# A graph network on one core: rows for the aggregations fetched per block in edge order, or not at all

## The reference

```
h   = relu(layernorm(x))
agg = segment_sum(h[src], dst)            # 1st aggregation
h2  = relu(agg / max(cnt, 1) @ W1l.T + b1 + h @ W1r.T)
agg = segment_sum(h2[src], dst)           # 2nd aggregation
x   = x + agg / max(cnt, 1) @ W2l.T + b2 + h2 @ W2r.T
h   = relu(layernorm(x))
x   = x + segment_mean(relu([h[src], h[dst], e] @ W1 + b1) @ W2 + b2, src)   # edge layer
```

## Time and profile before

| | us |
|---|---|
| three runs | 4372.95, 4394.75, 4398.56 |
| median | 4394.75 |
| span of the profiled execution | 4375.3 |

### The profile page before, as it was taken

How to read it: one execution, slowest core, us unless ns; L and a number is a source line. 1 busy time by engine, 2 the same in 40 slices (tenths; PEclk the granted TensorE clock), 3 DMA queues, 4 the chain that set the end, 5 groups by cost and what they waited for, 6 DMA issues and landing times. The chain is left out here.

```text
span 4375.3 us, 174335 instructions
## 1 busy us (share of the span) xinstructions
PE 3697.5 (85%) x64703; PEld 3536.1 (81%) x64703; DVE 3679.1 (84%) x6413; ACT 2589.0 (59%) x5168; POOL 3032.7 (69%) x2760
## 2 busy tenths in 40 slices
PE   3699999999977999999758888888888888888876
PEld 3688888888877999999747887877788887788876
DVE  7799999999988888888758888887878878888876
ACT  3455555555545666666537666666666666666664
POOL 1688888888854666666517777777777777777771
PEclk9899999999999999999868999999999999999998
DMA  5233333333326545555335555555555555555552
GB/s 104 68 84 83 83 82 83 83 83 85 82 64 170 118 118 118 118 118 119 68 110 162 163 169 175 174 159 159 164 166 174 174 162 161 160 165 174 174 153 65
DMA packets 481209, 557.42 MB, mean 127 GB/s; under 512 B 180610, under 2 KB 437873, under 8 KB 480870
## 3 DMA queue, kind: packets, MB, share of 16 engines
q1 hardware_dynamic: 395782, 451.91, 36.7%
q0 software_dynamic: 84032, 103.47, 10.2%
q10 hardware_dynamic: 1266, 0.31, 0.0%
HBM read 478.48 MB, written 76.90 MB: 127 GB/s over the span
## 5 line engine op out<-in xcount | busy, mean ns | idle before, releaser
L1388 POOL DMA_INDIRECT sorted_edges<-edge_rows,edge_index x1566 | 1535.3, 980 | 568.0 <-issue 559.1
L969 POOL DMA_INDIRECT conv_got<-parts_table,conv_index x1060 | 1324.5, 1250 | 467.2 <-issue 235.7
L1079 ACT CAST conv_rows<-conv_rows_ps 128x384 bf16<-128x384 f32 x2226 | 1020.3, 458 | 671.4 <-PE conv_rows_ps L993 654.8
L993 PE MATMUL conv_rows_ps<-parts,conv_hot_t 128*128 128x192 bf16 x8268 | 1049.8, 246 | 72.4 <-DVE conv_hot_t L1145 72.4
L1010 PE MATMUL conv_sums<-conv_rows,conv_hot_d 128*128 128x193 bf16 (+1 forms) x8268 | 1052.6, 247 | 3.0 <-DMA conv_got<-parts_table,conv_index 3.0
L993 PEld LDWEIGHTS conv_rows_ps<-parts,conv_hot_t 128*128 128x128 bf16 x8268 | 696.4, 97 | 94.7 <-issue 55.4
L1450 PE MATMUL edge_sums<-edge_parts,edge_hot 128*128 128x64 bf16 (+1 forms) x15582 | 597.2, 200 | 201.0 <-DVE acc L1640 196.7
L1450 PEld LDWEIGHTS edge_sums<-edge_parts,edge_hot 128*128 128x128 bf16 x15582 | 556.8, 102 | 220.9 <-DVE acc L1640 165.0
L1010 PEld LDWEIGHTS conv_sums<-conv_rows,conv_hot_d 128*128 128x128 bf16 x8268 | 720.4, 98 | 4.2 <-DMA conv_got<-parts_table,conv_index 3.7
L1435 PE MATMUL edge_a_ps<-parts,edge_hot_t 128*128 128x64 bf16 x15582 | 548.7, 197 | 36.4 <-issue 25.3
L1145 DVE TENSOR_SCALAR conv_hot_t<-conv_slot_row,node_of 128x768 bf16<-128x768 bf16 (+1 forms) x1484 | 542.1, 407 | 22.0 <-PE conv_rows_ps L993 14.6
(11 more groups left out here) (193 smaller groups left out, 4717.5 us busy)
## 6 DMA issues: line engine op xcount, KB each, us to landing
edge_slot_row<-slot_rows SPq DMA_DIRECT2D x371, 224.0 KB
edge_edges<-sorted_edges SPq DMA_DIRECT2D x371, 224.0 KB
conv_slot_row<-slot_rows SPq DMA_DIRECT2D x424, 192.0 KB
conv_slot_row<-slot_rows SPq DMA_DIRECT2D x318, 160.0 KB
edge_dst_row<-dst_rows SPq DMA_DIRECT2D x261, 192.0 KB
edge_attr<-in_edge_attr SPq DMA_DIRECT2D x260, 192.0 KB
sorted_edges<-edge_rows,edge_index POOLq DMA_INDIRECT x1566
conv_got<-parts_table,conv_index POOLq DMA_INDIRECT x1060
```

The costliest lines, as they stand in the source:

```text
L969: pool.indirect_dma_start(got[g][:, f, 0:PARTS * D], None, k.parts_table, bass.IndirectOffsetOnAxis(ap=index[h][:, g, at:at + 1], axis=0)) ...
L993: mm = pe.matmul(rows_ps[(bs * h + i) % banks][:, at:at + PARTS * D], hot_t[home[g]][:, v, u * P:(u + 1) * P], k.parts[:, 2 * (GU * g + u) ...
L1079: act.copy(rows[i % bufs][:, 0:n, 0:PARTS * D], rows_ps[(bs * h + i) % banks][:, 0:n * PARTS * D].rearrange("p (u d) -> p u d", u=n)).then ...
L1388: pool.indirect_dma_start(k.sorted, bass.IndirectOffsetOnAxis(ap=index[h][0:used, at:at + 1], axis=0), rows[j][0:used, t, :], None).then_i ...
```

## The change

Blocks are of two kinds. In a block of kind P no rows are fetched: all 49 units are expanded by PE. In a block of kind F nothing is expanded: GpSimd fetches all 3,840 rows by 30 indirect DMAs, one for each tile of 128 edges in their original order, and PE only reduces, 60 matmuls. `WHOLE` gives the pattern: conv1 alternates P, F (27 and 26 blocks), conv2 goes P, P, F (36 and 17 blocks). For an F block `hot_d` is made from `picked`, the destination numbers in edge order with those of unslotted edges set to zero. `index` holds all row numbers of the F blocks, made by two DVE instructions at the start; the fetches have five `got` tiles of seven, seven, seven, seven and two rows of tiles, each in one buffer that comes free when its group of the F block before has been reduced. In conv1 those tiles, `index` and `picked` lie in the room of `k.x`, and SP loads that part of x anew (72 of 98 windows) at the end. Sorting goes on for every block. The loops run over six blocks; POOL's stream is written out without a loop.

The diff, cut to its core:

```diff
-FETCHED = 2
+WHOLE = {"conv1": "PF", "conv2": "PPF"}
+ROUND = 6
@@ Sorting
+    def choose_dst(self, dve, c, f, picked):
+        k = self.k
+        link(dve, dve.scalar_tensor_tensor(self.at[:], self.rank[:], float(SRC_WINDOWS), k.src_window[:, bass.ds(c, 1), :].rearrange("p c t -> p (c t)"), ALU.mult, ALU.add), self.at_made, f + 1)
+        dve.scalar_tensor_tensor(picked[:, bass.ds(f, 1), :].rearrange("p f t -> p (f t)"), self.at[:], float(SLOTS),
+                                 k.dst_no[:, bass.ds(c, 1), :].rearrange("p c t -> p (c t)"), ALU.is_lt, ALU.mult).then_inc(self.dst_chosen, 1)
@@ conv
-        fetched = [1 + g % 2 for g in range(NG)]
-        steps = [[(u, min(u + 2, GU - n)) for u in range(0, GU - n, 2)] for n in fetched]
-        bs, cut, banks, bufs, most = NG * ns, 8, 2 if sorting else 3, 3, (GU - min(fetched)) * P
+        steps = [(u, min(u + 2, GU)) for u in range(0, GU, 2)]
+        bs, cut, banks, bufs = NG * ns, 10, 2 if sorting else 4, 4
...
+        room = k.x[:].rearrange("p w d -> p (w d)").bitcast(BF16)[:, 0:of_x] if sorting else o.tmp("room", [P, of_x], BF16)[:]
+        got = [room[:, g * a_got:(g + 1) * a_got].rearrange("p (u d) -> p u d", u=GU) for g in range(WG)]
@@ sync
+                if sorting:
+                    s.store_row(sp, t.b)
+                if t.kind == "F":
+                    return
...
+            if sorting:
+                sp.wait_ge(s.row_stored, 16 * NB)
+                sp.wait_ge(reduced, Turn(kinds, whole[-1]).made + WG)
+                sp.dma_start(k.x[:, 0:x_taken, :], k.x_rows[:, 0:x_taken, :]).then_inc(x_back, 16)
+                sp.wait_ge(x_back, 16)
@@ gpsimd
-            def number_rows(b, h, n):
...
+            pool.wait_ge(begun, 2)
+            pool.wait_ge(index_made, 1)
+            for f, b in enumerate(whole):
+                for g in range(WG):
+                    if f >= 1:
+                        pool.wait_ge(reduced, Turn(kinds, whole[f - 1]).made + g + 1)
+                    for t in tiles_of(g):
+                        pool.indirect_dma_start(got[g][:, t - GU * g, 0:PARTS * D], None, k.parts_table, bass.IndirectOffsetOnAxis(ap=index[:, f, t:t + 1], axis=0)).then_inc(got_landed[g], 16)
@@ tensor
+            def reduce_whole(t, g):
+                pe.wait_ge(hot_d_made, t.made + g + 1)
+                pe.wait_ge(got_landed[g], 16 * len(tiles_of(g)) * (t.f + 1))
+                if g == 0:
+                    sums_free(t)
+                for x in tiles_of(g):
+                    mm = add_up(t, g, x - GU * g, got[g][:, x - GU * g, 0:wide_cols])
+                mm.then_inc(reduced, 1)
...
+                for i in range(cut):
+                    if t.kind == "P":
+                        expand(t, i)
+                    if i < 2 and t.n >= 1 and last.kind == "P":
+                        rest_of(last, bs - 2 + i)
+                    if i >= 2 and t.kind == "P":
+                        reduce(t, i - 2)
+                    if i in (3, 8) and t.kind == "F":
+                        reduce_whole(t, i // 5)
+                    hooks(i, last, t, t1, t2)
+            def second(last, t, t1, t2, t3):
+                for j in range(3):
+                    if t.n >= 0 and t.kind == "F":
+                        reduce_whole(t, 2 + j)
+                    if j < 2 and sorts(t2) and (t.n < 0 or t.kind == "F"):
+                        s.prefix(pe, t2.b, t2.n, 1 + j)
@@ vector
+            at = slice(whole[0], NB, len(kinds))
+            link(dve, dve.scalar_tensor_tensor(node, k.src_window[:, at, :], float(SW), k.src_no[:, at, :], ALU.mult, ALU.add), node_made, 1)
+            dve.tensor_scalar(index, node, 1.0, float(ROWS - 1), ALU.subtract, ALU.min).then_inc(index_made, 1)
             if not sorting:
-                units = k.slot_src[:].rearrange("p b (g u) -> p b g u", u=GU)[:, :, :, GU - FETCHED:GU]
-                dve.tensor_tensor(row_of[:], units, wide(k.first_row[:], 1, [P, NB, NG, FETCHED]), ALU.add).then_inc(rows_numbered, 1)
+                dve.scalar_tensor_tensor(picked, k.place[:, at, :], float(SLOTS), k.dst_no[:, at, :], ALU.is_lt, ALU.mult).then_inc(all_picked, 1)
```

More of the change, by code:

```diff
@@ L906, in in_turn, with at @@
-            for b in range(2 * pairs, NB):
-                second(b, b % 2, MANY)
-                if b + 1 < NB:
-                    first(b + 1, (b + 1) % 2, MANY)
-        def sorts(b, lag):
-            return sorting and (not isinstance(b, int) or 0 <= b + lag < NB)
+            def at(c, i=None):
+                return [Turn(kinds, c + d, i) for d in (-1, 0, 1, 2, 3)]
+            for c in range(-ahead, 1):
+                first(*at(c))
+                if c < 0:
+                    second(*at(c))
@@ new lines, in in_turn, with here @@
+            second(*at(0))
+            first(*at(1))
+            second(*at(1))
+            first(*at(2))
+            with eng.Fori(0, rounds) as i:
+                for r in range(ROUND):
+                    second(*at(2 + r, i))
+                    first(*at(3 + r, i))
+            for c in range(2 + ROUND * rounds, NB):
+                second(*at(c))
+                if c + 1 < NB:
+                    first(*at(c + 1))
+        def here(t):
+            return not t.known or 0 <= t.b < NB
@@ new lines, in sums_free, with add_up @@
+            def sums_free(t):
+                if t.n >= 2:
+                    pe.wait_ge(summed, t.b - 1)
+            def add_up(t, g, u, row):
+                for v in range(2):
+                    mm = pe.matmul(sums[t.h][:, v * wide_cols:(v + 1) * wide_cols], hot_d[home_d[starts[t.c % len(kinds)] + g]][:, u, v * P:(v + 1) * P], row,
+                                   start=(g == 0 and u == 0 and v == 0), stop=(GU * g + u == t.units - 1), skip_group_check=True)
+                return mm
@@ L1069, in _ @@
+            in_turn(pe, first, second)
+            last = Turn(kinds, NB - 1)
+            if last.kind == "P":
+                for i in (bs - 2, bs - 1):
+                    rest_of(last, i)
+            move(last)
             if sorting:
@@ L1154, in take, with make_hot @@
-            def take(b, h, n):
-                dve.wait_ge(reduced, NG * b + NG)
-                dve.tensor_scalar(moved_to[:], k.iota[:], k.shift_to[:, bass.ds(b, 1)], None, ALU.is_equal)
-                both = sums[h][:, 0:2 * wide_cols].rearrange("p (v d) -> p v d", v=2)
+            def make_hot(t, g):
+                if t.kind == "P":
+                    dve.wait_ge(landed[g], 16 * (t.p + 1))
+                    if not t.known or t.p >= 1 or g >= since[g]:
+                        dve.wait_ge(expanded, ns * (NG * t.p + g + 1 - since[g]))
+                    for v in range(2):
+                        last = dve.tensor_scalar(hot_t[home[g]][:, v, :], slot_row[lane[g]][:], k.node_of[:, v:v + 1], None, ALU.is_equal)
+                    last.then_inc(hot_t_made, 1)
+                if g == 0:
+                    dve.wait_ge(dst_ready, t.b + 1)
+                x = starts[t.c % len(kinds)] + g
+                if not t.known or t.made + g >= since_d[x]:
+                    dve.wait_ge(reduced, t.made + g + 1 - since_d[x])
+                same_number(dve, hot_d[home_d[x]], k.nodes_b[:] if sorting else nodes_ps[:, 0:SW // 2].bitcast(BF16), dst_of[t.h], g, t.units).then_inc(hot_d_made, 1)
@@ L1159, in take @@
+            def take(t):
+                dve.wait_ge(reduced, t.made + t.groups)
+                dve.tensor_scalar(moved_to[:], k.iota[:], k.shift_to[:, bass.ds(t.b, 1)], None, ALU.is_equal)
+                both = sums[t.h][:, 0:2 * wide_cols].rearrange("p (v d) -> p v d", v=2)
                 if sorting:
@@ new lines, in second @@
+            def second(last, t, t1, t2, t3):
+                for g in range(3, NG):
+                    if t.n >= 0 and g < t.groups:
+                        make_hot(t, g)
+                    if g - 3 in range(t2.sums) and sorts(t2):
+                        s.plane(dve, t2.b, t2.h, t2.n, g - 3, t2.sums)
+                    if g == 4 and t.n >= 1:
+                        add(last)
+                    if g == 4 and not sorting:
+                        add_bias(t)
+                    if g == 5 and sorts(t2):
+                        s.choose(dve, t2.b, t2.n)
+                    if g == 6 and sorts(t2):
+                        s.sum_chosen(dve, t2.b, t2.n)
+                    if g == 5 and sorting and t.known and t.b == NB - 2:
+                        s.put_places(dve)
+                if here(t1):
+                    make_hot(t1, 0)
+                if sorts(t2):
+                    s.spread_rank(dve, t2.b)
+                    if t2.kind == "F":
+                        s.choose_dst(dve, t2.b, t2.f, picked)
```

430 lines of the change are left out of this document (192 added, 238 removed).

## The result

The kernel after took 4418.36 us (median of 19 runs), the kernel before 4372.95 us (19 runs on the same chip). The ratio, formed over the runs and not from the two medians, is 1.0081 (95% interval 1.0063 to 1.0100): slower by 35 us, against the forecast of 83.

A forecast was written before the change was run, and what follows sets the result against it. PE and DVE together bound conv1 and PE alone conv2; POOL was to become conv1's chain. conv1 +173 and conv2 -90 sum to +83 us, added to the median 4394.75: 4478 us, range 4350 to 4600.

The forecast's parts named there:

- 200 + 25T: Forecast end of conv1 in us, with T the time of a pair of blocks: 1460 at T = 50.4.
- T: Time of a conv1 pair, one P and one F block, with POOL's 30 fetches as the chain: 50.4 us.
- 25T - 1177: Sum of the changes in conv1 (25T - 1087) and conv2 (-90): +83 us at T = 50.4.
- in between: Rival in conv1: T = 45.3 to 48.8, no change in time, 4395 us; chance 0.18.
- this gives a formula: Conv1 fetches start at random; mean wait is the sum of L²/2 over runs, over T: T = 50.4 us.
- fetches miss the runs: Rival in conv1: fetch starts aren't random; half the sum of runs gives T = 44.8, -57, 4338 us; chance 0.15.
- -90 forecast: conv2: PE bounds it, three blocks take 40 us, 714 us in all, -94 and +4 for the start.
- Fetch at 703.38 began inside a pair of hot_t and took 0.95: conv1 before: trace evidence taken against the skill's rule that 2-port perf modes lock out GpSimd; 0.95 us.
- hot_t holds fetches as well: Rival in conv1 and conv2: hot_t holds fetches too, T = 51.8, +35, and conv2 +32: 4545 us; chance 0.07.
- 33 to 35: Time in us that PE and DVE need for a conv1 pair when POOL doesn't bound it.
- The clock rival: Rival in conv1: PE idles in F blocks, its clock drops in P blocks, T about 55.5, +210, 4605 us; chance 0.10.
- nothing changes: Edge layer: its time was forecast to stay the same, 0 us.

The follow-up runs named there:

- e1: The kernel after, with the node numbers of conv1's hot_d read from PSUM, as conv2 does: 4324.2 us, ratio 0.9896 to before.
- e6: The kernel after, with rank prefixes, next one-hots and conv2's move of sums reordered in F blocks alone: 4391.4 us, ratio 1.0016 to before.
- e9: The kernel before, with the node numbers of conv1's hot_d read from PSUM: 4370.4 us, ratio 0.9996 to before.
- e2: The kernel after, with the pattern P, P, F in conv1 as well: 4334.6 us, ratio 0.9917 to before.
- e3: The kernel after, with only 17 of the 30 fetches of each conv1 F block issued: 4332.9 us, ratio 0.9883 to before.
- e10: As e8, but PPF in conv1, 24 blocks a pass in both loops, slot sums behind F blocks two steps later, DVE's conv1 order as in after: 4251.0 us.
- e5: The kernel after, with 24 blocks instead of 6 in a pass of conv2's loop: 4389.7 us, ratio 1.0011 to before.
- e8: The kernel after with the edits of e1 and e6, 2 blocks a pass in conv1's loop and 24 in conv2's: 4236.4 us, ratio 0.9660 to before.
- e4: conv1 as in the kernel before, conv2 as in the kernel after: 4355.6 us, ratio 0.9954 to before.

## Why the prediction was half right

**What bounds the kernel, and the new chain: right.** POOL became the chain of conv1 (after, e1, e6), PE stays the chain of conv2, and e9 shows that POOL had not bounded before. The end of conv1 was 200 + 25T in form: at T = 45.7 that gives 1343, measured 1346.0, which leaves little room for a cost of the reload of x.

**The sign: right by luck.** With the measured T of 45.7 the recorded sum 25T - 1177 gives -35 us, a faster kernel. Slower it was because conv2 gained 65.5 us less than forecast, and 26 of the 37.7 us between the two profiled spans lie in the last stage, which the change doesn't touch. T itself fell into the prediction's band "in between" (45.3 to 48.8, chance 0.18), not into the forecast's 48 to 53.

**The step that failed in conv1: "this gives a formula".** T = 37.5 + 30*21.7/T holds a mean wait of 0.43 us; it was 1.217 - 0.947 = 0.27. That is 30 x 0.16 = 4.8 us a pair, some 115 us in all, the whole of conv1's miss. The formula assumes that a fetch starts at a random moment and sits through the rest of an unbroken run of SBUF-only instructions. I took runs and waits from the trace of each kernel (300 to 1200 us; instructions less than 0.03 us apart make a run; the held share is the part of the time in which a two-input instruction runs; L is the length of a run or an instruction and T the stretch, so the two sums are the formula's mean wait in us; "waited" is what a fetch took over 0.95):

| | held share | sum L²/2T over runs | over single instructions | waited |
|---|---|---|---|---|
| before | 0.62 | 0.58 | 0.32 | 0.58 |
| after | 0.52 | 0.65 | 0.27 | 0.27 |
| e2 | 0.57 | 0.63 | 0.29 | 0.50 |
| e3 | 0.56 | 0.70 | 0.29 | 0.23 |
| e1 | 0.28 | 0.19 | 0.13 | 0.08 |
| e9 | 0.29 | 0.19 | 0.13 | 0.04 |
| e10 | 0.28 | 0.19 | 0.13 | 0.19 |

By runs it fits in the kernel before and in e10 alone; e9 and e10 have the same sums and waited 0.04 and 0.19. In the kernel before every block repeats to 0.1 us, so it was one phase seen 42 times, not a sample of random ones; after is not held more than before, and waited half as long. The timelines of after show what the formula leaves out (POOL, then DVE):

```profile
625.53 1.49 POOL L1027 DMA_INDIRECT x<-parts_table,x  x1 [0.30 <-issue]
627.33 1.44 POOL L1027 DMA_INDIRECT x<-parts_table,x  x1 [0.30 <-issue]
629.07 1.57 POOL L1027 DMA_INDIRECT x<-parts_table,x  x1 [0.30 <-issue]
...
650.19 3.13 POOL L1027 DMA_INDIRECT x<-parts_table,x  x1 [0.30 <-issue]
```

```profile
624.65 1.56 DVE L773 TENSOR_TENSOR conv_slot_hot<-iota_b,conv_rank_quads 128x1280 bf16<-128x1280 bf16 x2
626.12 1.08 DVE L150 TENSOR_TENSOR conv_hot_d<-nodes_b,conv_dst_of 128x1792 bf16<-128x1792 bf16 x1
627.13 0.82 DVE L773 TENSOR_TENSOR conv_slot_hot<-iota_b,conv_rank_quads 128x1280 bf16<-128x1280 bf16 x1
627.86 0.96 DVE L674 TENSOR_TENSOR conv_member<-iota_b,conv_number 128x1560 bf16<-128x1560 bf16 x1
628.74 1.08 DVE L150 TENSOR_TENSOR conv_hot_d<-nodes_b,conv_dst_of 128x1792 bf16<-128x1792 bf16 x1
...
649.79 0.80 DVE L1218 TENSOR_SCALAR conv_hot_t<-conv_slot_row,node_of 128x896 bf16<-128x896 bf16 x2
650.51 1.08 DVE L150 TENSOR_TENSOR conv_hot_d<-nodes_b,conv_dst_of 128x1792 bf16<-128x1792 bf16 x1
651.51 0.96 DVE L686 TENSOR_TENSOR conv_planes<-conv_member,conv_number 128x1560 bf16<-128x1560 bf16 x1
```

DVE's two-input instructions run without a break from 624.65 to 629.8. The fetches at 625.53 and 627.33 end 0.82 after 626.20 and 627.95: they came through at the first boundary between two instructions. The one at 650.19 began inside a `hot_t`, before L150 started, and did not: it ends 0.85 after 652.47, behind the `hot_t`, L150 and L686. So a run is sometimes one lock and sometimes several. What decides it the runs don't settle, and it isn't the pair of instructions alone: at the boundary from L766 to L674 (L773 to L674 in after) all 42 waiting fetches stayed held in before, and all 40 came through in after. No kernel in the table waited over 0.01 us more than its sum by runs; three (e3, e1, e9) waited less than their sum over single instructions. So the sum by runs was an upper bound here, and no estimate. By single instructions the lengths in the earlier trace rows give 12.2 instead of 21.7 for a pair, and T = 45.5. That it comes so near the measured 45.7 is one case: e2 waited nearly twice its sum over single instructions, e3 and e1 less than theirs. The 45.5 is close to the rival "fetches miss the runs" at half weight (T = 44.8), to which I gave 0.15, though its reason was another one.

**conv2: -90 forecast, -24.5 measured.** The matmul count and the hiding of the fetches were right (0.977 us each, POOL waits for PE). Three terms of the sum failed. PE's stops at the F block, allowed at 0.6 us: a triple took 41.8 us and not 40, 17 x 1.8 = 31 us, of which e6's new order gave back 19.4. The returns of a loop whose body grew from two blocks to six, put at nothing: 7 returns of 3.3 us, 23 us, of which e5 removed six for 19.8. And the block of before, read as 15.25 us: that window of the earlier trace rows holds 186 matmuls, where the stage has 9540 in 53 blocks, 180 each, and the adds of before are 15.0 us apart, so there were 13 us less to win. Together that is 67 us; the miss was 65.5. e8 has both edits and is 46 us below after, at -70.5 against before.

**"Fetch at 703.38 began inside a pair of hot_t and took 0.95": wrong as a proof.** The two `tensor_scalar` are two instructions, and a fetch may get in between. In conv2 of the kernel before, where no other SBUF-only instruction runs (POOL, then DVE):

```profile
1700.58 1.01 POOL L969 DMA_INDIRECT conv_got<-parts_table,conv_index  x1 [0.30 <-issue]
1705.65 1.06 POOL L969 DMA_INDIRECT conv_got<-parts_table,conv_index  x1 [0.30 <-issue]
```

```profile
1700.36 0.75 DVE L1145 TENSOR_SCALAR conv_hot_t<-conv_slot_row,node_of 128x768 bf16<-128x768 bf16 x2
1705.16 0.74 DVE L1145 TENSOR_SCALAR conv_hot_t<-conv_slot_row,node_of 128x768 bf16<-128x768 bf16 x2
```

Both fetches end 0.82 us behind the end of one of the two halves, at 1700.77 and 1705.89. The rule of the Trainium skill that I had set aside ("SBUF — State Buffer", "SBUF: two separate sides": a 2-port perf mode takes the lock too, and the lock is held for the whole instruction) holds in these two. It costs them little, 0.06 to 0.11 us. In conv1 of after it costs more: 60 of the 593 fetches between 300 and 1200 us were held though no two-input instruction ran in their first 0.13 us, each by a `hot_t`. 41 of them came through behind it and waited 0.17 us on average; the other 19, as the one at 650.19, stayed behind L150 and L686 too and waited 2.2 us each. The 60 hold 48 of the 160 us waited in all. So the rival "hot_t holds fetches as well" was right in its mechanism, and I had given it 0.07; its price of 67 us above the forecast did not come.

**PE's and DVE's floor of the pair, "33 to 35": wrong, and hidden by POOL.** It was 42.4 (e3). About 1.1 of that are returns of the loop. I counted busy time; the F block turned a chain that PE's own work had covered into a wait, and the wait into a slow clock. The clock rival had the mechanism at a smaller size: PE is slow for 6.7 us after the F block, not for a whole P block, at a cost of up to 3.4 us a pair. That lies behind POOL's chain in after, and in the open as soon as POOL is relieved (e1 to e3).

**The edge layer, "nothing changes": -18.7 us.** It is a row of 1566 fetches on POOL, 1535.3 us busy and 980 ns each before, 1517.1 and 969 after. Every kernel with the old conv1 shows 977 to 980 (before, e4, e9), every other 967 to 970. The fetched rows are the same; I don't know the cause.

## What to carry to other kernels

A rule fitted to a kernel that repeats one phase has been tested once, however many rows it has: look in the trace for a case that breaks it (the conv2 rows of before had some) before a change is priced by it. When blocks of a loop become unequal, follow each wait of the short block along its whole chain, since the cover that it had was the long block's work; and count what the new body size does at the loop's return. When relieving an engine doesn't move the time, relieve the next one together with it: here the new order gave conv1 nothing by itself (e6), PSUM by itself ran into the next chain after 2.6 us a pair (e1), and with the returns gone as well conv1 and conv2 together are 156 us shorter than in after (e8).
